# Flamingo block on one core: layer 1's q projected transposed for two tiles at a time, instead of in rows with four turnings per tile

## The reference: what is computed

```python
x = x + tanh(g_xattn[0]) * L0_xattn(layernorm(x), ctx, ...)   # 32 heads of 128, 8 kv heads, RMS norm on q and k
x = x + tanh(g_ffn[0])   * L0_ffn(layernorm(x), ...)          # 8 LoRA experts, softmax router
x = x + tanh(g_xattn[1]) * L1_xattn(layernorm(x), ctx, ...)   # 16 heads of 96, 4 kv heads, no norm
x = x + tanh(g_ffn[1])   * L1_ffn(layernorm(x), ...)          # gated MLP, 1792 wide
```

```python
q = (latents @ Wq.T).reshape(b, q_len, H, HD)                  # H = 16, HD = 96
k, v = hidden @ Wk.T, hidden @ Wv.T                            # hidden = [context, latents], 256 rows per sequence
scores = einsum('bkgqd,bksd->bkgqs', q, k) / sqrt(HD)
out = einsum('bkgqs,bksd->bkgqd', softmax(scores), v)          # then reshaped and @ Wo.T
```

## Time and profile before

| | us |
|---|---|
| median of three runs | 1293.63 (1289.31 to 1296.59) |
| the profiled execution, device time | 1291.96 |
| its span, first to last instruction | 1290.1 |
| PE busy | 1254.1 (97%) |
| DVE busy | 962.0 (75%) |
| ACT busy | 830.8 (64%) |
| POOL busy | 582.9 (45%) |

### The profile page before, as it was taken

How to read it: one execution, slowest core, us unless ns; L and a number is a source line. 1 busy time by engine, 2 the same in 40 slices (tenths; PEclk the granted TensorE clock), 3 DMA queues, 4 the chain that set the end, 5 groups by cost and what they waited for, 6 DMA issues and landing times.

```text
span 1290.1 us, 24439 instructions
## 1 busy us (share of the span) xinstructions
PE 1254.1 (97%) x7392; PEld 1103.9 (86%) x7392; DVE 962.0 (75%) x2425; ACT 830.8 (64%) x2867; POOL 582.9 (45%) x1029
## 2 busy tenths in 40 slices
PE   8799999999999999999999989999999999999998
PEld 7698888888888888888888878899999999878886
DVE  7778777867787787787778888887777778963434
ACT  6677777767777777787778655576666666632221
POOL 3566555556565565566555642332333323540000
PEclk9899999999999999999999999999999999999999
DMA  6465465554455654544655431333543324370000
GB/s 211 92 131 115 83 135 105 113 110 103 102 115 103 130 106 95 123 109 86 134 113 101 102 71 34 69 72 70 103 91 66 85 57 101 73 179 1 33 1 33
DMA packets 339078, 121.11 MB, mean 94 GB/s; under 512 B 307104, under 2 KB 325280, under 8 KB 338976
## 3 DMA queue, kind: packets, MB, share of 16 engines
q1 hardware_dynamic: 313888, 84.59, 34.3%
q10 hardware_dynamic: 21104, 29.12, 7.9%
q0 software_dynamic: 3984, 6.29, 2.0%
HBM read 39.21 MB, written 2.10 MB: 32 GB/s over the span
## 4 chain that ended last, share of the span: by engine, by line
PE 52%; DVE 17%; ACT 14%; issue 5%; POOL 5%; DMA 5%; SPq 0%; ACTq 0%; DVEq 0%; POOLq 0%
PE bank L575 13%; PE bank L577 13%; PE bank L576 13%; PE bank L816 7%; DVE split L1217 5%; DMA turned<-scratch 4%; PE bank L834 4%; DVE scratch L1291 3%; ACT scratch L941 3%; POOL rq L1666 3%; ACT scratch L916 3%; ACT bank L904 3%; DVE mx L1300 2%; ACT pieces L953 2%; PE bank L670 1%
## 5 line engine op out<-in xcount | busy, mean ns | idle before, releaser
L575 PE MATMUL bank<-split 128*128 128x256 f32 (+6 forms) x2120 | 704.0, 332 | 19.5 <-DVE split L1217 8.3
L576 PE MATMUL bank<-split 128*128 128x256 f32 (+6 forms) x2120 | 692.4, 327 | 0.0
L577 PE MATMUL bank<-split 128*128 128x256 f32 (+6 forms) x2120 | 692.4, 327 | 0.0
L575 PEld LDWEIGHTS bank<-split 128*128 128x128 f32 (+2 forms) x2120 | 403.0, 190 | 67.1 <-DVE split L1217 19.1
L577 PEld LDWEIGHTS bank<-split 128*128 128x128 f32 (+2 forms) x2120 | 402.7, 190 | 34.7
L576 PEld LDWEIGHTS bank<-split 128*128 128x128 f32 (+2 forms) x2120 | 403.3, 190 | 30.8
L1647 POOL CAST split<-turned 128x512 fp32r<-128x512 f16 x384 | 234.5, 640 | 289.0 <-DMA turned<-pieces 287.8
L870 ACT ACTIVATE split<-bank 96x256 fp32r<-96x256 f32 (+6 forms) x392 | 165.2, 432 | 81.4 <-PE bank L670 43.8
L1217 DVE TENSOR_TENSOR split<-bank,split 96x256 fp32r<-96x256 f32 (+6 forms) x392 | 185.4, 475 | 26.4 <-ACT split L870 20.1
L941 ACT ACTIVATE scratch<-bank,nb,w_max 128x256 f32<-128x256 f32 x256 | 141.5, 563 | 73.0 <-DVE nb L1303 72.8
L953 ACT ACTIVATE pieces<-scratch,rs 128x256 f16<-128x256 f32 x384 | 171.7, 509 | 8.7 <-DVE rs L1315 7.3
(11 more groups left out here) (82 smaller groups left out, 1268.7 us busy)
## 6 DMA issues: line engine op xcount, KB each, us to landing
raw<-in_wq_a ACTq DMA_DIRECT2D x14, 512.0 KB, 4.2
raw<-in_wo_a ACTq DMA_DIRECT2D x14, 512.0 KB, 3.8
raw<-in_wkv_a ACTq DMA_DIRECT2D x7, 512.0 KB, 6.7
turned<-pieces SPq DMA_TRANSPOSE x192, 3.3
raw<-in_wq_c ACTq DMA_DIRECT2D x8, 384.0 KB, 3.4
craw<-in_ctx_t SPq DMA_DIRECT2D x8, 256.0 KB, 3.5
raw<-in_wo_c ACTq DMA_DIRECT2D x4, 512.0 KB, 3.8
split<-in_down_t POOLq DMA_DIRECT2D x2, 1024.0 KB, 5.8
```

Of the source, the lines that this page charges most:

```text
L575: pe.matmul(out, whi, mhi, start=start, stop=False)
L576: pe.matmul(out, whi, mlo, start=False, stop=False)
L577: return pe.matmul(out, wlo, mhi, start=False, stop=stop)
```

## The change

`q_proj` and `q_turn` are no longer used for layer 1. `q_turned` multiplies with the weight as the stationary operand and 256 tokens (two tiles) as the moving one, so that q comes out transposed. It runs once for two tiles, in steps with b even, at the place of `q_proj`, and for tiles b+2 and b+3 (before: b+3). The weight columns of a group are put in three chunks of 128: the 96 columns of head c, then 32 of head 3's columns. So each of three outputs holds one head and a third of head 3. ACT and DVE take the high and low parts out in five pieces each (`qT_moves`), the last three of which move 32 partitions. The weight split is in two pieces per 384 columns (3x96 and 3x32).

The core of the diff, with its helper functions:

```diff
+        def q_block(L, w, k):
+            block = flat(w)[:, k * L.qw:(k + 1) * L.qw]
...
+            by_chunk = chunks(block, L.oc)
+            return [by_chunk[:, :, 0:L.hd], by_chunk[:, :, L.hd:P]]
...
+        def qT_moves(L):
+            rest = P - L.hd
+            first, last = chunks(bank[6][:, :], 2), bank[3][:, 0:2 * P]
+            heads = [(slice(0, L.hd), slice(0, 2), first[0:L.hd].rearrange("p c (s q) -> p c s q", s=2)),
+                     (slice(0, L.hd), slice(2, 3), last[0:L.hd].rearrange("p (c s q) -> p c s q", c=1, s=2))]
+            for c, src in enumerate((first[L.hd:P, 0, :], first[L.hd:P, 1, :], last[L.hd:P, :])):
+                heads.append((slice(rest * c, rest * (c + 1)), slice(L.oc, NH),
+                              src.rearrange("p (c s q) -> p c s q", c=1, s=2)))
+            return heads
...
+            def q_turned(L, g, b):
...
+                    pe.wait_ge(s.qlo_done, two_tiles(g, b, 0))
...
+                for c in range(L.oc):
+                    out = bank[6][:, c * 2 * P:(c + 1) * 2 * P] if c < 2 else bank[3][:, 0:2 * P]
+                    for k in range(KC):
...
+                        at_c = k * L.qw + c * P
+                        last = mm3(out, tuple(flat(w)[:, at_c:at_c + P] for w in wq),
+                                   at(xT, slice(None), k, slice(tile * P, (tile + 2) * P)),
+                                   start=k == 0, stop=k == KC - 1)
+                last.then_inc(s.q_done, 1)
...
-            def q_turn(L, g, b):
...
@@ scores
-                    pe.wait_ge(s.qlo_done, count(g, b, 1, 1))
+                    pe.wait_ge(s.qlo_done, two_tiles(g, b, 1))
@@ PE step
-                if three is not None:
+                if three is not None and three[0] is L0:
                     q_proj(*three)
+                if three is not None and three[0] is L1 and three[2] % 2:
+                    q_turned(*two)
...
-                if three is not None and three[0] is L1:
-                    q_turn(*three)
@@ ACT
-            def q_evac(L, g, b):
...
             def qt_evac(L, g, b):
                 s = attn[L.name]
-                act.wait_ge(s.qt_done, count(g, b, 1, 1))
-                copy(flat(qT[b % 2][0])[0:L.hd, :], bank[6][0:L.hd, :]).then_inc(s.qthi_done, 1)
+                act.wait_ge(s.q_done, g * (NT // 2) + (b // 2 + 1))
+                for rows, heads, src in qT_moves(L):
+                    copy(qT_two[rows, 0, heads], src).then_inc(s.qthi_done, 1)
@@ DVE
-                low(flat(qT[b % 2][1])[0:L.hd, :], bank[6][0:L.hd, :], flat(qT[b % 2][0])[0:L.hd, :]
-                    ).then_inc(s.qlo_done, 1)
+                for rows, heads, src in qT_moves(L):
+                    low(qT_two[rows, 1, heads], src, qT_two[rows, 0, heads]).then_inc(s.qlo_done, 1)
@@ ACT and DVE step
-                if three is not None and three[0] is L1:
-                    qt_evac(*three)
+                if three is not None and three[0] is L1 and three[2] % 2:
+                    qt_evac(*two)
...
-                    qt_low(*three)
+                if three is not None and three[0] is L1 and three[2] % 2:
+                    qt_low(*two)
```

More of the change, by code:

```diff
@@ L38 @@
 VS = 4
+QT_OPS = 5
 KV = 2 * SEQ
@@ L87, in __init__ @@
         else:
[L88 to L89 removed]
+            self.qthi_done, self.qlo_done = sem("qthi_done"), sem("qlo_done")
             self.kt_done, self.khi_done, self.klo_done = (sem(n) for n in ("kt_done", "khi_done", "klo_done"))
@@ L177, in new_weights, with two_tiles @@
             group if b == NT - 4 else None)
+def two_tiles(g, b, more):
+    return g * (NT // 2 * QT_OPS) + (b // 2 + more) * QT_OPS
 def starts(g, b):
@@ L251, in build @@
         qT = [pair(NH * P, NH) for _ in range(2)]
+        qT_two = split[:, qT_at:spot[0]].rearrange("p (s w h q) -> p w h s q", s=2, w=2, q=P)
         wq_at = spot[0]
@@ L630, in kv_proj @@
                     last.then_inc(s.kv_done, 1)
+            def q_turned(L, g, b):
+                s = attn[L.name]
+                gb, tile = g + b // NT, b % NT
+                if starts(g, b):
+                    pe.wait_ge(attn[L0.name].qb_done, NH * L0.tiles)
+                else:
+                    pe.wait_ge(s.qlo_done, two_tiles(g, b, 0))
+                if is_at(L, g, L1, 0) and b < NT:
+                    pe.wait_ge(norm[2].lo, tile + 2)
+                for c in range(L.oc):
+                    out = bank[6][:, c * 2 * P:(c + 1) * 2 * P] if c < 2 else bank[3][:, 0:2 * P]
+                    for k in range(KC):
+                        if tile == 0 and c == 0 and k == 3:
+                            pe.wait_ge(s.wq_lo, (gb + 1) * L.qp)
+                        if tile == 0 and c == 0 and k < 3:
+                            pe.wait_ge(s.wq_lo_rest, (gb * 3 + (k + 1)) * L.qp)
+                        at_c = k * L.qw + c * P
[3 more added lines that the diff above has]
+                last.then_inc(s.q_done, 1)
             def q_proj(L, g, b):
@@ L634, in q_proj @@
                 gb, tile = g + b // NT, b % NT
[L635 to L644, removed]
+                if is_at(L, g, L0, 0) and b <= 3:
+                    if b >= 2:
+                        pe.wait_ge(s.qb_done, NH * (2 if b == 2 else 1))
+                elif not starts(g, b):
+                    pe.wait_ge(s.qb_done, count(g, b, NH, 0))
                 if is_at(L, g, L0, 0) and b < NT:
                     pe.wait_ge(norm[0].lo, tile + 1)
-                if is_at(L, g, L1, 0) and b < NT:
-                    pe.wait_ge(norm[2].lo, tile + 1)
                 for k in range(KC):
@@ L973, in q_hi @@
                 act.wait_ge(s.in_q, g * 32 + 32)
-                sl = slice(k * L.qw, (k + 1) * L.qw)
-                copy(flat(wq[0])[:, sl], raw_q[:, sl]).then_inc(s.wq_hi, 1)
+                for out, in_ in zip(q_block(L, wq[0], k), raw_q_block(L, k)):
+                    copy(out, in_).then_inc(s.wq_hi, 1)
             def o_hi(L, g, c):
@@ L1065, in step @@
                 else:
-                    if three is not None:
-                        q_evac(*three)
                     if three is not None and two is not None and two[0] is L1:
@@ L1095, in load_staged @@
                 if b == 1:
-                    act.wait_ge(s.wq_lo, L1.groups)
-                    act.wait_ge(s.wq_lo_rest, L1.groups * 3)
+                    act.wait_ge(s.wq_lo, L1.groups * L1.qp)
+                    act.wait_ge(s.wq_lo_rest, L1.groups * 3 * L1.qp)
                     act.dma_start(staged[0][0], gate_src[:, :, 0:4 * P]).then_inc(in_ff[0], 16)
@@ L1381, in q_lo @@
                 s = attn[L.name]
[L1382 to L1385, removed]
+                dve.wait_ge(s.wq_hi, (g * KC + (k + 1)) * L.qp)
+                for out, in_, hi in zip(q_block(L, wq[1], k), raw_q_block(L, k), q_block(L, wq[0], k)):
+                    low(out, in_, hi).then_inc(s.wq_lo_rest, 1)
             def step(L, g, b):
@@ L1630, in q_lo @@
                 s = attn[L.name]
-                sl = slice(k * L.qw, (k + 1) * L.qw)
-                pool.wait_ge(s.wq_hi, g * KC + (k + 1))
-                part_low(flat(wq[1])[:, sl], raw_q[:, sl], flat(wq[0])[:, sl]).then_inc(s.wq_lo, 1)
+                pool.wait_ge(s.wq_hi, (g * KC + (k + 1)) * L.qp)
+                for out, in_, hi in zip(q_block(L, wq[1], k), raw_q_block(L, k), q_block(L, wq[0], k)):
+                    part_low(out, in_, hi).then_inc(s.wq_lo, 1)
             def o_lo(L, g, c):
@@ L1799, in _ @@
             cast_probs(L1, g, NT - 1, 1)
-            pool.wait_ge(attn[L1.name].q_done, L1.tiles)
+            pool.wait_ge(attn[L1.name].q_done, L1.tiles // 2)
             pool.dma_start(down_mid, down_src[:, MD:ME, :]).then_inc(in_ff[2], 16)
```

21 lines of the change are left out of this document (12 added, 9 removed).

## The result

The changed kernel takes 1337.61 us (median of four runs, 1333.38 to 1343.26), against 1292.38 in the runs beside it: 1.035 times as long, with a 95% interval of 1.030 to 1.040. The forecast was slower, 1325 in 1303 to 1341. By the medians that is 45 us more, where the forecast had 31. The profiled execution is the fastest of the four: 1333.38, 41 more than the one of before, where the sum had said 32.

A forecast was written before the change was run, and what follows sets the result against it. PE's own work was taken to bound layer 1. Pairs +22.9 (16 at 1.43), weight splits +6.9 and the last group +1.8 gave +31.6, on 1291.96 1323.6; forecast 1325 with the median's offset, range 1303 to 1341.

The forecast's parts named there:

- The bound of 0.29: Lower bound for each DVE q piece moving 32 partitions, from the 32x128 form; the forecast took 0.42.
- Points 2, 3 and 4: Short-step PE waits, 0.7 each: scores for q's low part, k_turn for k rows, the next step's kv_proj for k_low.
- 42 us of PE waiting: Expected waits for DVE: 16 x 2.1 in short steps, 6.9 for weight splits, 1.8 in the last group.
- the costlier rival: Short steps: DVE's chain meets POOL's casts, 0.6 each, 10 us more in all: 1335; chance 0.12.
- one of the prediction's own signs of being wrong: Layer 1's granted clock falling under 0.98 would show the prediction wrong.
- +2.3 three times: Step 5 of three groups: DVE's low parts of the next weights, no longer covered by q_proj, +6.9 in sum.
- it costs more: DVE instructions slowed by POOL's casts in each short step, 10 us more: 1335; chance 0.12.
- delay two short steps by 0.9: Last group: the layernorm's statistics on DVE lie between y_add and o_low, +1.8 in sum.
- The clock could add to it: Layer 1, with PE as busy as in a stretch at clock 0.97: 3% of some 340 us, 10 us.
- The cover that was costed at nothing: ACT's five pieces, beside 4.32 of projection in long steps, and POOL's casts for values in short steps: no cost.
- Half of it: Short steps: k_low in time, only two waits bind, 8.8 to 9.2 long; 1306 to 1314; chance 0.16.
- It gets faster: DVE clears its tail between y_add and k_low in time; PE keeps its 10.9 gain, 1283; chance 0.07.

The follow-up runs named there:

- the second experiment: The kernel before the change with layer 1's four q transposes per tile left out: 1279.37 us, 0.989 of before.
- the filled step: The changed kernel with idle transposes filling PE's waits in short steps of layer 1's middle groups: 1333.15 us, 1.031 of before.
- the first and fourth experiment: The first: the changed kernel with the three pieces that move 32 partitions left out on ACT and DVE: 1316.96 us, 1.018 of before.
- The fourth experiment: The changed kernel reordered on ACT and DVE, so that q's low parts are made before y_add instead of behind it: 1313.52 us, 1.016 of before.
- the last run: The changed kernel with q's pieces earlier, the next q weights' low parts on POOL, one output-weight low part fewer ahead of the cast: 1304.88 us, 1.008.

## Why the prediction was right

**What bounds, and the bare sizes.** The long step was forecast at 12.10 and measured at 12.08; the short one at 9.9 and 9.77. The q pieces on DVE were taken at 2.4; the ten low parts from 938.40 on take 4.31, less the 1.90 of the other five that is 2.4. The 32x256 one has a mean of 427 ns between 853 and 1099 us. The bound of 0.29 for it was not needed: the elements counted, the partitions did not. PE's gain of 0.41 per tile for the turning is 0.40 in the second experiment.

**The three waits.** Points 2, 3 and 4 expected 0.7 each. They read 0.57, 0.49 and 0.34, 1.40 in place of 2.1, and yet the step is 9.77 long as forecast. An idle entry starts where the matmul ahead is over, not where the next would have started: 0.28 - 0.12 = 0.16 later for 256 columns. Three times 0.16 is 0.5, and 1.9 against 9.77 - 7.78 = 2.0 closes the step. So a wait's price is read from the length of the step, not from the idle entry. For the whole, the prediction named 42 us of PE waiting. In the three stages PE was idle for 34.6 (385.98 less 351.42 busy), against 3.0 before; with 0.16 for each of the 39 waits, some 41.

**The sum.** Forecast +31.6, measured +41.4 between the profiled executions, and +45 between the medians. By stages: the entry 3 x 1.43 = 4.3 forecast, 6.0 measured. The middle 10 x 1.43 + 6.9 = 21.2 forecast, 27.5 measured. The last group, with long steps at +1.82, short ones at -0.38 and one layernorm among them, 3 x 1.82 - 2 x 0.38 + 0.9 = 5.6 forecast, 8.9 measured. The mechanism was right, but two terms were too small and a third, the clock, was not in the sum. The result lies in the upper part of the range, which reached to 1341 only because of the costlier rival; it is above that rival's own 1335. And one of the prediction's own signs of being wrong came: layer 1's granted clock fell under 0.98, to 0.94 to 0.96.

The first is "+2.3 three times" for the weight split: a step 5 was to be 12.2, and is 14.81, 13.56 and 14.02, 13.1 over three plain ones where the sum had 6.9. DVE's timeline of the one that took 13.56, and what POOL and ACT did:

```profile
960.35 0.61 DVE L1255 TENSOR_TENSOR split<-raw,split 128x288 fp32r<-128x288 f32 x2
...
963.30 1.20 DVE L1255 TENSOR_TENSOR split<-raw,split 128x288 fp32r<-128x288 f32 x2
...
966.08 0.90 DVE L1255 TENSOR_TENSOR split<-raw,split 128x288 fp32r<-128x288 f32 x2
...
967.61 1.28 DVE L1343 TENSOR_REDUCE nb<-bank 128x2 f32<-128x512 f32 x2
```

```profile
963.03 1.36 POOL L1657 TENSOR_TENSOR split<-raw,split 128x288 fp32r<-128x288 f32 x2 [2.82 <-ACT split L916]
```

```profile
969.24 0.52 ACT L916 ACTIVATE split<-raw 128x384 fp32r<-128x384 f32 x1
```

The three low parts take 0.61, 1.20 and 0.90, 2.7 for the 2.4 of the sum. The same pair of instructions takes 0.61 alone and 1.20 beside POOL's: that is the contention of the rival "it costs more". The Trainium skill (GPSIMD Engine Reference, Key points), cited there, names VectorE instructions with two SBUF inputs; these have two, raw and split, and the trace agrees. Row_max starts at 967.61, 8.1 behind the step's start, for 7.8 forecast. Then ACT has a copy of the k and v weights between the exponentials (969.24), which the sum had left out, and k_low ends 4.7 after row_max's start instead of 4.38. These two, 8.1 and 4.7, make up 12.8 of the 12.96 of the filled step; the clock makes the rest, 0.6 to 1.1 where it was tried.

The second is the last group's "delay two short steps by 0.9". The step at 1121.52 took 14.75 for 10.8. It has a wait that the sum did not have, the layernorm's scale behind row_max, for which PE's turning of it waits:

```profile
1129.65 0.69 PE L638 MATMUL bank<-ident,scratch 128*128 128x128 f32 x2 [1.23 <-DVE scratch L1277]
```

and its granted clock was 0.77.

The clock was in the prediction only as part of that rival ("The clock could add to it"), and cost nothing in the forecast. Of the 10 that were missed, 3 are shown to be the clock's by the filled steps (1.4, 0.6, 1.1). The steps at 808.84, 865.35 and 1121.52, at 0.81, 0.77 and 0.77, were not filled, so their part stays open. An estimate from the windows: 0.04, 0.04 and 0.06 of the three stages' 90.49, 233.62 and 61.87 us is some 17 us of missing clock, an upper bound, since part of it falls on PE's waits. With the waiting near its forecast, the clock is a likely cause of much of the rest, but no run shows it. In the step 1 above, PE's matmuls of 512 columns read:

```profile
922.60 0.63 PE L614 MATMUL bank<-split 128*96 128x512 f32 x1
923.03 0.63 PE L612 MATMUL bank<-split 128*128 128x512 f32 x1
...
924.08 0.40 PE L612 MATMUL bank<-split 128*128 128x512 f32 x1
924.31 0.39 PE L613 MATMUL bank<-split 128*128 128x512 f32 x1
```

Until 923.5 they start 0.43 apart, which is 512 columns at 1.2 GHz, then 0.23 apart at 2.4 GHz; ahead of them PE had waited 0.56 at scores and 0.49 at k_turn. The Trainium skill (TensorE: Matmul & The Clock Gate, Back-to-back issue gap) has a gap of N / 1.2 ns for the cold clock, 427 ns for 512 columns; the trace agrees with its 0.43.

**The cover that was costed at nothing.** ACT's five pieces did stay free in plain steps. POOL's casts did so only while DVE's chain was longer: in the first and fourth experiment, with that chain shortened, values waited 1.6 for the cast in step 1. In the last run, with one low part less ahead of the cast, that wait was 0.37.

**The rivals.** "Half of it" fell: k_low was late, and the short step was 9.77, not 8.8 to 9.2. "It gets faster" needed a short step under 8.46. The fourth experiment got 8.17 by another order, and its plain pair was indeed 0.29 under the 20.56 of before; the change's own order did not reach it. "It costs more" was true in the steps 5, by contention and by the clock; in the plain short step shown neither did, and a step 1 lost 1.4 to the clock.

## What to carry to other kernels

When work of the bounding engine is bunched into every second step, look at the short step: the bunched work was the cover for what the other engines do in every step, and what they do because of it (here five pieces of q) must not stand behind the instruction that waits for the long step's end (here y_add). Where an engine idles just ahead of a row of work that others wait for, try whether that row can go into the idle time; here it was worth 24 us. Where PE's waits come thick, put a term for the clock into the sum: here it cost 1.4 behind two waits of 1.05 in sum, 0.6 and 1.1 in two steps 5, and nothing in other steps with waits as long.

## What the runs showed of the hardware

The granted clock fell in steps where PE waited several times, and not in others with the same waits: the steps from 937.54 (waits of 0.57, 0.49 and 0.34) and from 1007.08 (0.57 and 0.49) had a clock of 1.00, the one from 914.29 had 0.56 and 0.49 at 0.85. Filling the waits with transposes of no use brought it to 1.00 and made the step 1.4 shorter. What tells these steps apart stays open: the ones from 914.29 and 1007.08 are the same step of two groups, with the same instructions. A DVE low part on 32 partitions by 256 elements takes 427 ns, on 96 partitions 415 (means between 853 and 1099 us), so moving a head in three pieces costs three times as much on DVE as moving it whole.
